# Lead of the row gathers, lag of the row scatters, and a scratch write on Pool, in a kernel of attention and a mixture of experts

## What is computed

```python
logits = -dist2 + jnp.einsum('bld,ed->ble', x, rw) + rb
topv, topi = jax.lax.top_k(logits, TOP_K)
w = jax.nn.softmax(topv, axis=-1)
hidden = jax.nn.gelu(jnp.einsum('bld,efd->blef', x, w1) + b1, approximate=False)
exp_out = jnp.einsum('blef,edf->bled', hidden, w2) + b2
fused = jnp.sum(w[..., None] * jnp.take_along_axis(exp_out, topi[..., None], axis=2), axis=2)
```

## Time and profile before

| | us |
|---|---|
| median of 3 runs | 700.9 |
| lowest and highest run | 699.55, 707.57 |
| span of the profiled execution | 694.4 |
| the expert steps, from the first gelu to the last y_add | 239.0 to 664.3 |
| the tail behind them (last scatters, sums, output) | 664.3 to 694.4 |

### The profile page before, as it was taken

One profiled execution on the slowest core, in us unless ns is written; L12 is line 12 of the kernel. 1 busy time (PEld: TensorE's weight loads), 2 busy tenths in 40 slices (PEclk: granted clock), 3 DMA queues, 4 the chain that ended last, 5 costly groups with the idle time before them and its releaser, 6 DMA issues.

```text
span 694.4 us, 19926 instructions
## 1 busy us (share of the span) xinstructions
PE 536.4 (77%) x6242; PEld 481.6 (69%) x6242; DVE 364.9 (53%) x1325; ACT 353.7 (51%) x1079; POOL 281.1 (40%) x308
## 2 busy tenths in 40 slices
PE   4999879994502789977678789789977776679984
PEld 4967779993401489976677679678967776668942
DVE  6554779997999356545434553112334432233126
ACT  6524167775556365546445667336634434335513
POOL 4000000000451543566666743664566666645520
PEclk9999999998655799999999999999999989989998
DMA  8970000006001455444444645445866644546553
GB/s 229 255 280 9 3 3 0 0 0 243 1 1 76 120 161 157 138 131 131 131 140 143 204 124 162 135 144 146 264 207 180 183 130 133 145 122 192 174 197 122
DMA packets 55746, 92.28 MB, mean 133 GB/s; under 512 B 10352, under 2 KB 26096, under 8 KB 55152
## 3 DMA queue, kind: packets, MB, share of 16 engines
q1 hardware_dynamic: 45424, 72.35, 35.0%
q0 software_dynamic: 10240, 18.89, 9.2%
HBM read 78.07 MB, written 17.37 MB: 137 GB/s over the span
## 4 chain that ended last, share of the span: by engine, by line
PE 43%; issue 18%; DVE 18%; POOL 8%; ACT 7%; DMA 2%; DVEq 2%; another core or an unknown queue 0%; POOLq 0%; SPq 0%; ACTq 0%
PE bank L2148 15%; PE bank L2141 13%; POOL yd L600 6%; ACT value L883 3%; DVE shared L1187 2%; DVE shared L1179 2%; POOL shared L592 2%; DVE early L1467 2%; PE bank L1735 2%; DMA shared<-yd 1%; PE bank L1772 1%; PE bank L1840 1%; PE bank L1762 1%; PE bank L2133 1%; PE bank L2089 1%
## 5 line engine op out<-in xcount | busy, mean ns | idle before, releaser
L883 ACT ACTIVATE value<-bank,shared 128x128 f32<-128x128 f32 x632 | 180.8, 376 | 203.0 <-PE bank L2141 156.7
L2148 PE MATMUL bank<-shared,value 128*128 x1264 | 182.7, 290 | 62.4 <-ACT value L883 41.7
L2148 PEld LDWEIGHTS bank<-shared,value 128*128 128x128 f32 x1264 | 161.7, 200 | 76.7 <-issue 76.1
L2141 PE MATMUL bank<-early,shared 128*128 x1264 | 180.9, 288 | 5.3 <-issue 2.8
L592 POOL DMA_INDIRECT shared<-xd,early x128 | 125.5, 980 | 127.5 <-PE bank L2141 79.8
L2141 PEld LDWEIGHTS bank<-early,shared 128*128 128x128 f32 x1264 | 162.6, 200 | 9.3 <-issue 8.4
L1663 DVE SCALAR_TENSOR_TENSOR early<-bank,value,early 128x128 f32 x158 | 55.4, 351 | 195.8 <-PE bank L2148 116.6
L600 POOL DMA_INDIRECT yd<-early x128 | 128.3, 1002 | 67.8 <-DVE early L1663 36.2
L560 POOL TENSOR_TENSOR shared<-shared,xn 128x512 f32<-128x512 f32 x4 | 5.1, 1264 | 174.9 <-DVE xn L1262 167.1
L2133 PE MATMUL bank<-ident,shared 128*128 128x128 f32 x128 | 35.9, 284 | 9.0 <-DMA shared<-xd,early 5.7
L2003 PE MATMUL bank<-ksp,shared 128*128 128x32 bf16 x1536 | 40.9, 177 | 0.0
(11 more groups left out here) (334 smaller groups left out, 689.3 us busy)
## 6 DMA issues: line engine op xcount, KB each, us to landing
shared<-w1b SPq DMA_DIRECT2D x158, 258.0 KB
w1b<-in_w_t SPq DMA_DIRECT2D x1, 4096.0 KB, 17.8
shared<-col_dram SPq DMA_DIRECT2D x1, 4096.0 KB, 13.4
shared<-in_w_t SPq DMA_DIRECT2D x1, 4096.0 KB, 12.3
att<-yd SPq DMA_DIRECT2D x8, 512.0 KB
shared<-yd SPq DMA_DIRECT2D x4, 1024.0 KB, 9.1
xd<-xnT SPq DMA_DIRECT2D x2, 1280.0 KB
shared<-xd,early POOLq DMA_INDIRECT x128
```

What stands on the lines that cost most here:

```text
L883: ins = act.activation(hT[:, i % 2, tok(c)], bank[2 + i % 2][:, tok(c)], ACT.Gelu, bias=w1_now[:, i % WR, F + c:F + c + 1])
L2141: ins = mm(bank[2 + i % 2][:, tok(c)], w1_now[:, i % WR, tok(c)], x_now, start=True, stop=True)
L2148: ins = mm(bank[6 + i % 2][:, 0:D], hT[:, i % 2, tok(c)], w2_sb[:, bass.ds(e, 1), c, :] .rearrange("p a d -> p (a d)"), start=(c == 0), st ...
```

## The change

Three things are changed, all on Pool's queue. `NEAR` goes from 8 to 16: gather n may be issued when up of the step 16 before is done, and the first 16 gathers wait for no step. `BEHIND` goes from 27 to 34: scatter n - 34 stands behind gather n. And a new helper `pause()` writes zeros to a scratch tile and waits for that write; it stands behind the gathers that have no scatter behind them, 34 in the first half (tiles 0 to 33) and 21 in the second (77 to 97).

```diff
-    BEHIND = 27
+    BEHIND = 34
...
-    NEAR = 8
+    NEAR = 16
...
+        pause_to = sb("pause_to", [P, P // 2])
...
+            pauses = [0]
+
+            def pause():
+                pool.memset(pause_to[:, :], 0.0).then_inc(paused, 1)
+                pauses[0] += 1
+                pool.wait_ge(paused, pauses[0])
+
...
-            for n in range(JT):
+            for n in range(BEHIND):
                 rows(n)
-                if n >= BEHIND:
-                    results(n - BEHIND)
+                pause()
+            for n in range(BEHIND, JT):
+                rows(n)
+                results(n - BEHIND)
...
             for n in range(JT + BEHIND_2, JT + BEHIND):
                 rows(n)
+                pause()
```

More of the change, by code:

```diff
@@ L321, in sandwich_kernel @@
         out_ready, out_done = sem("out_ready"), sem("out_done")
+        paused = sem("paused")
         block = ctx.enter_context(nc.Block())
```

## The result

The change made the kernel slower: 710.6 us median (12 runs, 707.06 to 715.72) against 702.3 for before beside it (12 runs, 699.52 to 707.57), a ratio of 1.012 with a 95% interval of 1.009 to 1.0155. The forecast was 690.4 and faster. The same kernel was measured four times more (e10, e15, e17, e18), with ratios of 1.010 to 1.019.

The account below looks back on a forecast made before the run. TensorE's signals were taken to be held while Pool issues DMAs back to back, making steps beside pairs about 1.1 us dearer. Terms -15.6 + 1 + 2.3 + 0 + 1.8 = -10.5 gave 690.4 us, range 680 to 711.

Parts of the forecast that it names:

- the price of a pair: Steady stretches: a step costs about 1.1 us more where Pool issues a gather and a scatter together.
- Fewer pairs, −15.6: Each half: 30 pairs for 37, seven steps go to scatters alone, saving 7.1 us in the first, 8.5 in the second.
- The start, +1: First gathers: pauses delay tile 5 by 1.7 us, partly hidden in gelu(1)'s hold; +1 us, between -2.4 and +5.
- Rival A: Pauses don't break the hold: start run +14.4, step 80 +5, sum +5.6 us or 706.5; chance 0.15.
- The pause: Gathers without a scatter: a gather with its scratch write takes 1.58 us, range 1.25 to 2.4.
- The first half's backlog, +2.3: At the first pair: Pool is 2.9 us or 1.2 pairs late after 34 gathers, catching up in a run; +2.3 us.
- The boundary, +1.8: Where the halves meet: a nine-DMA run costs 7.3 us, pairs ending at step 80 return 5.5; range -8.7 to +7.3.
- Sum: Whole kernel: -15.6 + 1 + 2.3 + 0 + 1.8 = -10.5 us, span 683.9, time 690.4.
- Rival C: The deep lead uncouples Pool and TensorE: pairs go at 2.57 us, 32 us more saved, 658; chance 0.08.

Follow-up runs that it names:

- e10: The changed kernel itself, unaltered, measured again on another chip; 703.7 us, ratio 1.010 to before.
- e15: The changed kernel itself, unaltered, measured again; 703.8 us, ratio 1.012 to before.
- e17: The changed kernel itself, unaltered, measured again; ratio 1.011 to before, which took 698.5 us.
- e18: The changed kernel itself, unaltered, measured again; ratio 1.019 to before, which took 699.1 us.
- e1: The changed kernel without pauses, its lead growing from 8 to 16 by one tile every two gathers in each half; 696.5 us, ratio 0.9958 to before.
- e16: The changed kernel without pauses and with the lead grown slowly from 8 to 16, measured again on another chip; 695.4 us, ratio 0.995 to before.
- e6: The changed kernel with five scratch writes, each waited for, in place of one in each pause; one run, 733.1 us beside 700.5.
- e12: The changed kernel with three waited-for scratch writes behind each of the first 16 gathers and no pause elsewhere; 706.1 us, ratio 1.015 to before.
- e2: The changed kernel without its pauses (scratch writes and waits); 704.7 us, ratio 1.0078 to before.
- e7: The changed kernel with the old lead of 8 and no pauses, BEHIND still 34; 666.4 us, ratio 1.034, where before took 645.1.
- e9: The changed kernel's lead 16 and BEHIND 34 in the first half only, second half as before, no pauses; 630.8 us, ratio 0.979, where before took 645.1.
- e8: The changed kernel with three waited-for scratch writes behind each of the first 16 gathers, no pause elsewhere; 616.2 us, ratio 0.954, where before took 645.1.
- e4: The changed kernel with BEHIND back at 27 and no pauses, so lead 16 alone; 738.3 us, ratio 1.0533 to before.
- e13: Lead 16 and BEHIND 34 in the first half only, no pauses, measured where signals are held; 700.0 us, ratio 1.002 to before.

## Why the prediction was wrong

The step that failed is this: "The 7 extra gathers alone cost no step, since the lead moves them 8 steps forward." It took the price of a pair (1.1 us a step) as a price of pairs. It is the price of a second Pool DMA in a step, whatever the DMA is. A deeper lead doesn't take gathers away, it brings them forward into steps that have theirs already, and each costs about 1 us there. The number of DMAs and of steps is the same in both kernels, so by this reading the account closes near zero at best. e1 and e16, half a per cent faster, are the best that was measured. e1 shows the price: 7 to 8 us paid while the lead grows, in each half, for 9 won later. The change pays more, because its extra DMAs come in unbroken runs.

Term by term, by the table above:

- **Fewer pairs, −15.6.** Right in place and nearly in size. Steps 48 to 57 took 21.3 us for 30.1 (−8.8; forecast −7.1), steps 126 to 135 24.6 for 33.6 (−9.0; forecast −8.5). Steps beside pairs stayed at 3.07 and 3.21.
- **The start, +1.** Wrong: +12.1 at step 2 and +13.1 at step 18, there +10.4 to +13.1 over five profiles, beyond the upper bound of +5. The bound left out that the run itself grows from 9 gathers to 18. Rival A had it, at +14.4.
- **The pause.** 1.39 us a gather, between the lower end of 1.25 and the 1.58 taken. The far end of 2.4, which the Trainium skill's rule (SBUF — State Buffer, the box on the "DVE blocks DMA" trap) spoke for, isn't seen: the 55 writes took 0.163 to 0.167 us. Of them 19 ran beside a VectorE operation and were no longer; whether one of those was in a two-port mode the trace doesn't tell. What mattered was not the price but that 0.44 us of quiet doesn't break the run; e6 and e12 show that 1.28 and 0.86 do.
- **The first half's backlog, +2.3.** +1.7 from step 18 to 48, near in size and by luck. At the measured 1.39 us a gather the same working ends 34 gathers at 277.7, ahead of the 281.2 that frees pair 34, so it gives no backlog; the other four profiles have +0.2 to +2.0 here, and e2, without pauses, +0.1.
- **The boundary, +1.8.** The run of nine DMAs, its place and its end came as forecast (11.3 us long, gelu 1.0 us behind its end; forecast 11.2 and 1.1), with +8.8 at step 71 (forecast 7.3). What was to come back, −5.5 behind step 80, did not: 4.1 us came back up to step 76, and then the five gathers alone that follow joined the last pairs in a run of ten DMAs, and from step 57 to 85 the sum is +13.9, above the upper bound of 7.3. Rival A named this run, at +5.
- **Sum.** −10.5 forecast, +13.5 measured from the first gather to the last step in this pair of profiles, +5.7 with e15 in the changed kernel's place, and +8.3 between the medians.

So rival A's mechanism came, the hold not broken by the pauses: 706.5 by its sum, 710.6 measured. Part of that nearness is luck: its boundary of +6.8 measured +13.9, and 4.7 of the 6.5 us that it added to the span are only that before's profiled execution was shorter than the median. It had been given 0.15. The evidence for it stood in the earlier trace rows, a hold of 2.42 us with gathers alone, and the one for the forecast was a guess that a wait for a write of Pool's own is more than a gap. Pauses that work don't save it, as e12 shows: there the hold at the start goes, and 12.8 us are lost again between step 5 and step 15, the ratio 1.015.

Rival C (signals no longer in the way, a win of tens of us) didn't come by the change. Something like it stands in e7 to e9, where nothing is held and before itself took 645.1.

What this doesn't settle: whether it is the chip that makes the difference, since the one chip without the hold was used once, for one set of runs, and no kernel was tried on it a second time; what the cause is, since the traces show the effect alone; and what the change itself does where nothing is held. All five measurements of it were made where signals are held. Its variant e8, the same orders with other pauses, gained 4.6% on the chip without it, and e9, half of it, 2.1%; that the change would win there too is likely and not shown. Where signals are held, the slow lead (e1, e16) is faster than before by half a per cent and than the changed kernel by 1.2% (e16 and e15, side by side); it wasn't run where they aren't.

## What to carry to other kernels

When one engine's signals are held behind another's back-to-back DMA work, count DMAs per step over the whole program before moving any: here moving one forward into a step that had one already cost about 1 us (e1). Putting DMAs earlier, or putting them off, turns into runs at the places where credit opens all at once (the start, a phase boundary, behind the last item of a kind), so look at those places first and not at the steady stretch. A short pause must be measured against the silence that is needed, and a schedule tuned around such a hold should be timed on more than one chip, since one kernel took 700 us on some and 645 on another here.

## What the runs showed of the hardware

- TensorE's semaphore increments reach ScalarE and Pool late while Pool issues indirect DMAs back to back. With 0.30 or 0.44 us between the DMAs a run holds them; with 0.86 (e12) or 1.28 us (e6) between them they pass, and Pool's memsets in the gap don't hold them.
- It is the increments themselves that are late, and TensorE's alone. A trace also records when each semaphore was raised (not every time is in the record). In the changed kernel, up(1) ends at 248.51 and its increment is recorded at 250.51, up(2) at 250.66 and 262.06, while ScalarE's copy that ends at 252.29, inside the same hold, has its increment at 252.30. Over the program 61 of 136 recorded increments of `up_ps` lie within 0.05 us of an up's end, but 124 of 125 of gelu's and 111 of 112 of y_add's. In e9 it is 155 of 156, 157 of 158 and 156 of 157.
- In the short runs beside pairs gelu mostly starts 0.8 to 1.3 us behind the run's last DMA. Behind the long ones it varies: 1.0 behind nine (the changed kernel, step 71), 2.3 behind eleven (e12), 3.4 behind 22 (e6), and once, in e2, 0.2 behind nine.
- The hold isn't complete: in long runs one signal now and then passes in the middle (gelu(1) of the changed kernel at 250.53, 2.0 us behind up; gelu(10) of e12 at 266.23), and a start run of 17 to 19 gathers cost between 6 and 12 us at step 2 (the changed kernel's five profiles, e2, e4, e13).
- It isn't always there. On the chips numbered 3, 14, 4, 0 and 8, and on that of the first measurement, before took 698 to 702 us and every trace shows the hold; in the one set of runs on number 10 it took 645.1, and runs of up to 135 Pool DMAs held nothing: no gelu starts more than 0.2 us behind its up but that of step 31, where ScalarE loads a table. That is 8% for the same program, more than any edit here won. That the chip is the cause is likely and not shown.
